# The softmax division of the second cross attention moves from GpSimd to VectorE, and the instruction orders from the experts on are new

## The chip, the cores and the metric

One Trainium2 chip, one core of it. The metric is the device time of the whole program in microseconds (us), median of the runs shown. The engines are TensorE (PE in the profile, PEld its weight loads), VectorE (DVE), ScalarE (ACT), GpSimd (POOL) and SyncE (SP).

## The reference

Sixteen sequences of 64 tokens with 128 features pass six blocks, each a layer norm, a function and a residual add. The context has 64 tokens of 96 features per sequence. The change touches the fifth block, whose function stands in full below.

```python
def reference(...):
    def _L1_xattn_ref(x, context, mask, W_q, W_k, W_v, W_o, b_o):   # HEADS = 8, DIM_HEAD = 64
        q = (x @ W_q).reshape(b, n, HEADS, DIM_HEAD)
        k = (context @ W_k).reshape(b, j, HEADS, DIM_HEAD)
        v = (context @ W_v).reshape(b, j, HEADS, DIM_HEAD)
        sim = jnp.einsum('bihd,bjhd->bhij', q, k) * scale
        sim = jnp.where(mask[:, None, None, :], sim, max_neg)
        attn = jax.nn.softmax(sim, axis=-1)
        out = jnp.einsum('bhij,bjhd->bihd', attn, v).reshape(b, n, INNER)
        return out @ W_o + b_o
    ...
    x = x + _L0_attn_ref(_layernorm(x, axis=-1), ...)    # causal attention, 16 heads
    x = x + _L0_xattn_ref(_layernorm(x, axis=-1), ...)   # cross attention, one head
    x = x + _L0_ffn_ref(_layernorm(x, axis=-1), ...)     # 8 experts (top 2) and a shared one
    x = x + _L1_attn_ref(_layernorm(x, axis=-1), ...)    # linear state recurrence, GELU, norm
    x = x + _L1_xattn_ref(_layernorm(x, axis=-1), ...)   # the function above
    x = x + _L1_ffn_ref(_layernorm(x, axis=-1), ...)     # 8 experts, each takes its best tokens
    return x
```

## The kernel before

The 1024 tokens are NT = 8 tiles of 128 rows, in two halves of HT = 4 tiles. `X` holds the residual stream, tile by tile, in SBUF, for the whole program; `XT` is the normalized input of a block, transposed. Every engine runs one list of steps, written out by hand at the end of its block (PE from L1100, ACT from L1569, DVE from L2132, POOL from L539), and each step waits on counting semaphores for what it needs. Nothing reorders these lists: a step that waits holds up every later step of its engine. Loads of weights are issued by SP long before they are used.

Every layer norm is spread over three engines: `ln_moments` (DVE, statistics of four tiles), `root` (POOL, the inverse root, L448), `ln_apply` (DVE, four tiles, L1828), `transpose_xn` (PE, L660) and `copy_xt` (ACT, L1380).

The second cross attention has, for each half, four `queries1` products (L970, copied by ACT at L1528 to `Q1T`), and for each tile t of the eight the following cycle:

1. `scores1` (PE): 4 products that write the mask bias (L988) and 32 small ones (L996) fill two PSUM banks; tile t waits until the maximum of tile t-2 is subtracted (`c_sub`).
2. `subtract_max1` (DVE): maximum of each row and head (L2030), then subtraction from PSUM into `Es` (L2033). `Es` has three buffers, so from t = 3 on the subtraction waits for the transposes of tile t-3 (`c_tr`).
3. `exponentials1` (ACT, L1532), in place in `Es`.
4. `probs1` (DVE): sums (L2041) and their reciprocal (L2042). It signals `c_sum`.
5. `weigh_probs` (POOL, L537): `Es` times the reciprocal, in place, 128 partitions by 512. It signals `c_prob`. Between tiles 2 and 3 POOL has `add_bias(0)` and `add_bias(1)` (L532), which add the output bias to the residual stream, once it is normalized (`xn_ready`).
6. `transpose_probs1` (PE, L1006, one bank), `copy_probs1` (ACT, L1538, into `PTs`), `weigh_values1` (PE, L1020), `copy_values1` (ACT, L1545, two copies into `V2`), `project_out` (PE, L1033, one bank) and `add1` (DVE, L2047), which waits for `bo_added` and releases the bank for the next tile.

After the eighth tile come the last layer norm and the second set of experts: `up1` (L1048), `gelu` (L1553), `down1` (L1060), `copy_ys` (L1561) and `add_expert` (DVE, L2119). Between them PE makes sixteen `count` products (L1087) for a search on DVE (`route`, from L2061) that finds which tokens an expert takes. `search_bits` (L2052) prepares shifted constants for it in half of `PTs`.

The program has `mask_row` (DVE, L1876) too, which turns the context mask into the row that L988 multiplies. It runs while the first experts compute.

Of the kernel before, what the change touches and what calls it, by code (L numbers as in the profile page):

```python
# [5 lines left out]
def decoder_kernel(nc: bass.Bass, w, out):  # L6
# [8 lines left out]
    ALU = mybir.AluOpType  # L15
# [41 lines left out]
    with ctx:  # L57
# [3 lines left out]
        def sem(name):  # L61
            return ctx.enter_context(nc.semaphore(name))

        def per_row(ap, n):

            return ap.unsqueeze(2).broadcast_to([ap.shape[0], ap.shape[1], n])
# [244 lines left out]
        c_sum = sem("c_sum")  # L311
# [132 lines left out]
        def _(pool):  # L444
# [89 lines left out]
            def weigh_probs(t):  # L534
                pool.wait_ge(c_sum, t + 1)
                e = Es[:, t % 3, :].rearrange("p (a s) -> p a s", s=S)
                nc.gpsimd.tensor_tensor(e, e, per_row(sm[:, t, 2, :], S), ALU.mult).then_inc(c_prob, 1)  # L537

# [82 lines left out]
            weigh_probs(0)  # L621
            weigh_probs(1)
            weigh_probs(2)
            add_bias(0)
            add_bias(1)
            weigh_probs(3)
            weigh_probs(4)
            weigh_probs(5)
            weigh_probs(6)
            weigh_probs(7)  # L630
# [6 lines left out]
        def _(pe):  # L637
# [252 lines left out]
            def up0_first(h, e):  # L890
                i = (E0 + 1) * h + e
                if i == 0:
                    pe.wait_ge(ld_f0, 128)
                    pe.wait_ge(kv_ready, 5)
                if e == 0:
                    pe.wait_ge(xt_ready[h], 3)
                if i >= 2:
                    pe.wait_ge(f_silu, i - 1)
                mm(bank[i % 2][:, :], W1a[:, e, :], XT[:, half(h)], start=True, stop=True).then_inc(f_h1, 1)  # L899

            def up0_third(h, e):
                i = (E0 + 1) * h + e
                if e == 0:
                    pe.wait_ge(xt_ready[h], 3)
                if i == 0:
                    pe.wait_ge(ld_f0, 128)
                    pe.wait_ge(a_sub, NU)
                if i == 1:
                    pe.wait_ge(kv_ready, 6)
                if i >= 2:  # L910
                    pe.wait_ge(f_h, i - 1)
                mm(bank[2 + i % 2][:, :], W3a[:, e, :], XT[:, half(h)], start=True, stop=True).then_inc(f_h3, 1)  # L912
# [42 lines left out]
            def read_out(h):  # L955
                pe.wait_ge(s_state[h], ROUNDS + 1)
                if h == 1:
                    pe.wait_ge(s_gelu[0], 1)
                mm(bank[6][:, :], ST[:, h, :, :].rearrange("p b s -> p (b s)"),
                   CT[:, :, :].rearrange("p q d -> p (q d)"), start=True, stop=True).then_inc(s_y[h], 1)  # L960
# [273 lines left out]
            up0_third(1, 6)  # L1234
            up0_first(1, 7)
            down0(1, 5)
            up0_third(1, 7)
            down0(1, 6)
            up0_first(1, 8)
            down0(1, 7)  # L1240
            up0_third(1, 8)
# [6 lines left out]
            read_out(0)  # L1248
            transpose_xn(3, 1, 6)
            keys_values1(9)  # L1250
# [3 lines left out]
            widen(1, 1)  # L1254
            widen(1, 2)
            keys_values1(11)
# [15 lines left out]
            transpose_probs1(0)  # L1272
            queries1(1, 1)
            queries1(1, 2)
            queries1(1, 3)
            scores1(3)
# [13 lines left out]
            project_out(3)  # L1290
            transpose_probs1(4)
            scores1(7)
            weigh_values1(4)
            transpose_probs1(5)
            project_out(4)
            transpose_probs1(6)
            weigh_values1(5)
            weigh_values1(6)
# [76 lines left out]
        def _(act):  # L1375
# [304 lines left out]
            weigh0(1, 3)  # L1680
            silu(1, 5)
            silu(1, 6)
            copy_xt(3, 0, 7)
            weigh0(1, 4)
            silu(1, 7)
            weigh0(1, 5)
            weigh0(1, 6)
            silu(1, 8)
# [3 lines left out]
            copy_xt(3, 1, 6)  # L1692
            state(1, 0)
            state(1, 1)
            keys_values1(8)
            keys_values1(9)
            state(1, 2)
# [6 lines left out]
            keys_values1(14)  # L1704
            copy_xt(4, 0, 0)
            queries1(0, 0)
            queries1(0, 1)
            keys_values1(15)
# [3 lines left out]
            copy_xt(4, 1, 6)  # L1712
            queries1(1, 0)
            copy_probs1(0)
            queries1(1, 1)
            exponentials1(1)
            queries1(1, 2)
            queries1(1, 3)
            exponentials1(2)
# [11 lines left out]
            copy_probs1(4)  # L1731
            copy_values1(4)
            copy_probs1(5)
            exponentials1(7)
            copy_probs1(6)
# [7 lines left out]
            copy_xt(5, 1, 6)  # L1743
            route_exp()
# [3 lines left out]
            copy_ys(0, 0)  # L1748
            copy_ys(0, 1)
# [3 lines left out]
            copy_ys(1, 0)  # L1753
            gelu(2, 0, 0)
            gelu(2, 1, 0)
            gelu(2, 0, 1)
# [36 lines left out]
        def _(dve):  # L1793
# [243 lines left out]
            def probs1(t):  # L2037

                dve.wait_ge(c_exp, t + 1)
                e = Es[:, t % 3, :].rearrange("p (a s) -> p a s", s=S)  # L2040
                then(V.tensor_reduce(sm[:, t, 1, :], e, AX.X, ALU.add))  # L2041
                V.reciprocal(sm[:, t, 2, :], sm[:, t, 1, :]).then_inc(c_sum, 1)  # L2042
# [132 lines left out]
            subtract_max(14)  # L2175
            subtract_max(15)
# [47 lines left out]
            mask_row()  # L2224
# [26 lines left out]
            probs1(0)  # L2251
            subtract_max1(1)
            subtract_max1(2)
            probs1(1)
# [13 lines left out]
            subtract_max1(7)  # L2268
            add1(4)
            ln_moments(5, 0)  # L2270
# [3 lines left out]
            add1(6)  # L2274
            add1(7)
            ln_moments(5, 1)
            ln_apply(5, 1)
            search_bits()
# [35 lines left out]
```

## Time and profile before

| | us |
|---|---|
| median of 3 runs | 254.05 |
| lowest and highest run | 252.47, 254.1 |
| the profiled execution, its own time | 255.0 |
| its span, first to last instruction | 253.3 |
| TensorE's mean granted clock over the span | 0.987 |

The span in forty slices of 6.3 us, as the page prints it (busy tenths of each engine; PEclk the granted clock in tenths of full speed):

```
PE   8997899889899999999988986999798999999995
DVE  5462899775949525454438999378755788778995
ACT  0756698943435859755862564575555635434360
POOL 4898900010200847439583122072411000000000
PEclk9999999999999999999999997699999999999999
```

A digit is the share of its slice in which the engine ran. The second cross attention lies at 155 to 188 us of the span, slices 25 to 30; the second experts follow to 247 us. Busy time of PE says that something was in its pipe, not that it ran at its peak. Of the idle times of the other engines only those count that a later step of PE had to wait for.

### The profile page before, as it was taken

Reading aid. Unit: us, or ns where it says so; the run is one execution under the profiler, and the core shown is the slowest. Engines: PE = TensorE matmul, PEld = TensorE weight load, DVE = VectorE, ACT = ScalarE, POOL = GpSimd, SP = SyncE. Lnnn points to the kernel's source line nnn. Section 1 sums busy time; section 2 is a strip of 40 time slices with the busy share of each in tenths; the row PEclk is TensorE's granted clock in tenths of the full one; section 3 lists DMA queues with packets and bytes.
Section 4 is the critical chain, followed back from the end, with each engine's and each line's share of the span. In section 5 each row is a group of like instructions: output and inputs, shape, how many; then the busy total and the mean of one; then the engine's idle time right before and its main releaser. Section 6 shows DMA issues by size and latency. Waiting matters only on the chain.

```text
span 253.3 us, 5539 instructions
## 1 busy us (share of the span) xinstructions
PE 233.2 (92%) x2018; PEld 158.3 (63%) x2018; DVE 172.1 (68%) x574; ACT 142.5 (56%) x297; POOL 79.0 (31%) x137
## 2 busy tenths in 40 slices
PE   8997899889899999999988986999798999999995
PEld 8555677654455666656664534497677575579765
DVE  5462899775949525454438999378755788778995
ACT  0756698943435859755862564575555635434360
POOL 4898900010200847439583122072411000000000
PEclk9999999999999999999999997699999999999999
DMA  5898950326700000000000000000000000000002
GB/s 135 174 199 243 308 153 27 107 83 169 211 0 0 5 0 0 1 0 3 0 1 3 1 0 3 0 3 5 1 3 1 3 0 0 0 4 0 3 0 83
DMA packets 22343, 12.23 MB, mean 48 GB/s; under 512 B 11320, under 2 KB 21309, under 8 KB 22317
## 3 DMA queue, kind: packets, MB, share of 16 engines
q1 hardware_dynamic: 21277, 11.53, 16.6%
q0 software_dynamic: 80, 0.20, 0.9%
q8 instruction: 16, 0.26, 0.4%
q10 hardware_dynamic: 960, 0.16, 0.3%
q14 instruction: 10, 0.08, 0.1%
HBM read 8.74 MB, written 3.15 MB: 47 GB/s over the span
## 4 chain that ended last, share of the span: by engine, by line
PE 37%; DVE 12%; POOL 2%; ACT 2%; issue 1%; DVEq 0%
PE bank L1048 11%; PE bank L1060 10%; PE bank L931 2%; PE bank L1033 2%; PE bank L970 2%; PE bank L912 2%; DVE stats L1806 2%; PE bank L899 1%; PE bank L1006 1%; PE bank L1020 1%; DVE sm L2030 1%; DVE XN L2006 1%; DVE XN L1828 1%; POOL Es L537 1%; POOL rs L448 1%
## 5 line engine op out<-in xcount | busy, mean ns | idle before, releaser
L448 POOL TENSOR_TENSOR rs<-rs,halves 128x4 f32<-128x4 f32 x14 | 14.3, 1023 | 78.2 <-DVE rs L1821 62.3
L524 POOL TENSOR_TENSOR X<-X,att 128x128 f32<-128x128 f32 x72 | 30.7, 464 | 13.0 <-ACT att L1513 13.0
L1048 PE MATMUL bank<-XT,Wb 128*128 128x512 f32 x64 | 29.6, 597 | 0.0
L1981 DVE SCALAR_TENSOR_TENSOR att<-bank,cols,att 128x512 f32<-128x512 f32 x18 | 13.5, 749 | 22.6 <-ACT att L1502 16.6
L1060 PE MATMUL bank<-Wb,att 128*128 128x128 f32 x224 | 27.4, 278 | 0.0
L1060 PEld LDWEIGHTS bank<-Wb,att 128*128 128x128 f32 x224 | 25.9, 192 | 1.5 <-issue 0.8
L1553 ACT ACTIVATE att<-bank 128x512 f32<-128x512 f32 x32 | 18.0, 600 | 8.3 <-PE bank L1048 8.0
L1513 ACT ACTIVATE att<-bank,comb 128x128 f32<-128x128 f32 x72 | 20.3, 381 | 4.0 <-PE bank L931 4.0
L931 PEld LDWEIGHTS bank<-W2a,att 128*128 128x128 f32 x144 | 18.2, 191 | 6.3 <-issue 4.3
L1502 ACT ACTIVATE att<-bank,cols 128x512 f32<-128x512 f32 x18 | 12.6, 699 | 12.8 <-DVE att L1981 7.4
L1561 ACT ACTIVATE big<-bank 128x512 f32<-128x512 f32 x14 | 8.4, 597 | 18.8 <-PE bank L1060 18.8
L931 PE MATMUL bank<-W2a,att 128*128 128x128 f32 x144 | 18.9, 278 | 0.0
L899 PE MATMUL bank<-XT,W1a 128*128 128x512 f32 x36 | 18.3, 603 | 0.0
L912 PE MATMUL bank<-XT,W3a 128*128 128x512 f32 x36 | 18.2, 595 | 0.0
L1828 DVE TENSOR_SCALAR XN<-X,mv,rs 128x128 f32<-128x128 f32 x48 | 14.1, 356 | 5.2 <-POOL rs L448 4.9
L1048 PEld LDWEIGHTS bank<-XT,Wb 128*128 128x128 f32 x64 | 11.3, 191 | 10.0 <-issue 8.4
L2119 DVE SCALAR_TENSOR_TENSOR X<-big,rt,X 128x128 f32<-128x128 f32 x56 | 15.4, 347 | 0.8 <-ACT big L1561 0.6
L537 POOL TENSOR_TENSOR Es<-Es,sm 128x512 f32<-128x512 f32 x8 | 8.3, 1044 | 17.6 <-DVE sm L2042 17.5
L1380 ACT ACTIVATE XT<-bank 128x512 f32<-128x512 f32 x12 | 7.2, 604 | 9.1 <-PE bank L660 9.1
L1916 DVE TENSOR_REDUCE mx<-bank 128x8 f32<-128x512 f32 x16 | 10.4, 684 | 2.0 <-PE bank L771 2.0
L1806 DVE BATCH_NORM_STATS2 stats<-X 128x6 f32<-128x128 f32 x48 | 10.4, 279 | 1.7 <-DMA X<-in_x 1.5
L660 PE MATMUL bank<-ident,XN 128*128 128x128 f32 x48 | 10.1, 308 | 1.3 <-ACT QKVT L1523 0.7
(229 smaller groups left out, 472.6 us busy)
## 6 DMA issues: line engine op xcount, KB each, us to landing
o_scratch<-big SPq DMA_DIRECT2D x2, 512.0 KB, 2.9
Wb<-in_L_ffn_W SPq DMA_DIRECT2D x1, 1024.0 KB, 5.4
Wb<-in_L_ffn_W SPq DMA_DIRECT2D x8, 128.0 KB, 5.2
X<-in_x SPq DMA_DIRECT2D x2, 256.0 KB, 3.0
k_scratch<-QKVT SPq DMA_DIRECT2D x1, 512.0 KB, 4.0
q_scratch<-QKVT SPq DMA_DIRECT2D x1, 512.0 KB, 5.2
Wb<-k_scratch SPq DMA_DIRECT2D x1, 512.0 KB, 4.4
v_scratch<-QKVT SPq DMA_DIRECT2D x1, 512.0 KB, 7.0
```

Source lines behind the costliest of these rows:

```text
L448: nc.gpsimd.tensor_tensor(rs[:, 0, cut], rs[:, 1, cut], halves[:, :], ALU.pow).then_inc(l_root[h], 1)
L524: nc.gpsimd.tensor_tensor(X[:, h * HT + t, :], X[:, h * HT + t, :], part0[:, i % 2, t, :], ALU.add).then_inc(f_acc, 1)
L899: mm(bank[i % 2][:, :], W1a[:, e, :], XT[:, half(h)], start=True, stop=True).then_inc(f_h1, 1)
L912: mm(bank[2 + i % 2][:, :], W3a[:, e, :], XT[:, half(h)], start=True, stop=True).then_inc(f_h3, 1)
L931: last = mm(bank[4 + i % 2][:, t * P:(t + 1) * P], hid0[:, i % 2, t * P:(t + 1) * P], W2a[:, e, :], start=not shared, stop=True, skip_grou ...
L1048: mm(bank[i % 4][:, :], W1b[:, e, f * P:(f + 1) * P], XT[:, half(h)], start=True, stop=True).then_inc(m_up, 1)
L1060: last = mm(bank[4 + h][:, t * P:(t + 1) * P], hid[:, e % 2, f, tile], W2b[:, e, f, :], start=(f == 0), stop=(f == F1 - 1))
L1513: AF(part0[:, i % 2, t, :], bank[4 + i % 2][:, t * P:(t + 1) * P], ACT.Copy, scale=comb[:, tt, e:e + 1]).then_inc(f_part, 1)
L1553: AF(hid[:, e % 2, f, half(h)], bank[i % 4][:, :], ACT.Gelu).then_inc(m_gelu, 1)
L1806: last = V.bn_stats(stats[:, t, :], src[:, t, :])
L1828: V.tensor_scalar(XN[:, t, :], X[:, t, :], mv[:, t, 0:1], rs[:, 0, t:t + 1], ALU.subtract, ALU.mult).then_inc(xn_ready[h], 1)
L2119: last = V.scalar_tensor_tensor(X[:, t, :], ys[:, e, t, :], rt[:, 9, t, e:e + 1], X[:, t, :], ALU.mult, ALU.add)
```

## The change

In the cycle of a tile, step 5 disappears from POOL, and `probs1` on DVE gets a third instruction: it waits for the reciprocal (`then`) and multiplies `Es` by it, and signals `c_prob`. The semaphore `c_sum` goes. POOL's list then has the two `add_bias` steps directly behind `root(5, 1)`. The lists of PE, ACT and DVE are changed in their order in several places, without a step added or removed: among the last steps of the first experts, among the context's keys and values (`keys_values1(9)`, `(11)`, `(15)`), in the cycle of the second cross attention, and in ACT's first copies of the second experts (`copy_ys(0, 0)` and `(0, 1)`). DVE makes `mask_row` in the first attention, between the last two `subtract_max`, and `search_bits` before `add1(7)`.

```diff
--- before.py
+++ after.py
@@ -308,7 +308,6 @@
         c_sub = sem("c_sub")
         c_exp = sem("c_exp")
         bo_added = sem("bo_added")
-        c_sum = sem("c_sum")
         c_prob = sem("c_prob")
         c_tr = sem("c_tr")
         c_trc = sem("c_trc")
@@ -530,11 +529,6 @@
                 pool.wait_ge(xn_ready[h], 5 * HT)
                 rows = X[:, h * HT:(h + 1) * HT, :]
                 nc.gpsimd.tensor_tensor(rows, rows, per_col(bo[:, :], HT), ALU.add).then_inc(bo_added, 1)
-
-            def weigh_probs(t):
-                pool.wait_ge(c_sum, t + 1)
-                e = Es[:, t % 3, :].rearrange("p (a s) -> p a s", s=S)
-                nc.gpsimd.tensor_tensor(e, e, per_row(sm[:, t, 2, :], S), ALU.mult).then_inc(c_prob, 1)
 
             root(1, 0)
             root(1, 1)
@@ -618,16 +612,8 @@
             root(5, 0)
             root(4, 1)
             root(5, 1)
-            weigh_probs(0)
-            weigh_probs(1)
-            weigh_probs(2)
             add_bias(0)
             add_bias(1)
-            weigh_probs(3)
-            weigh_probs(4)
-            weigh_probs(5)
-            weigh_probs(6)
-            weigh_probs(7)
             root(6, 0)
             root(6, 1)
         C_MISC = 7 + E0 + 2 + 1 + 2
@@ -1232,13 +1218,13 @@
             up0_first(1, 5)
             up0_first(1, 6)
             up0_third(1, 6)
+            up0_third(1, 7)
+            down0(1, 5)
             up0_first(1, 7)
-            down0(1, 5)
-            up0_third(1, 7)
+            up0_first(1, 8)
             down0(1, 6)
-            up0_first(1, 8)
+            up0_third(1, 8)
             down0(1, 7)
-            up0_third(1, 8)
             inject(0)
             down0(1, 8)
             widen(0, 0)
@@ -1246,14 +1232,14 @@
             widen(0, 2)
             keys_values1(8)
             read_out(0)
+            keys_values1(9)
             transpose_xn(3, 1, 6)
-            keys_values1(9)
             inject(1)
             widen(1, 0)
             keys_values1(10)
             widen(1, 1)
+            keys_values1(11)
             widen(1, 2)
-            keys_values1(11)
             read_out(1)
             keys_values1(12)
             keys_values1(13)
@@ -1269,10 +1255,10 @@
             scores1(2)
             transpose_xn(4, 1, 6)
             queries1(1, 0)
-            transpose_probs1(0)
             queries1(1, 1)
             queries1(1, 2)
             queries1(1, 3)
+            transpose_probs1(0)
             scores1(3)
             weigh_values1(0)
             scores1(4)
@@ -1288,13 +1274,13 @@
             weigh_values1(3)
             scores1(6)
             project_out(3)
+            scores1(7)
             transpose_probs1(4)
-            scores1(7)
+            transpose_probs1(5)
             weigh_values1(4)
-            transpose_probs1(5)
-            project_out(4)
             transpose_probs1(6)
             weigh_values1(5)
+            project_out(4)
             weigh_values1(6)
             project_out(5)
             transpose_probs1(7)
@@ -1678,23 +1664,23 @@
             silu(1, 4)
             weigh0(1, 2)
             weigh0(1, 3)
+            copy_xt(3, 0, 7)
             silu(1, 5)
             silu(1, 6)
-            copy_xt(3, 0, 7)
             weigh0(1, 4)
+            weigh0(1, 5)
             silu(1, 7)
-            weigh0(1, 5)
+            silu(1, 8)
             weigh0(1, 6)
-            silu(1, 8)
             weigh0(1, 7)
             weigh0(1, 8)
             gelu_states(0)
             copy_xt(3, 1, 6)
+            keys_values1(8)
             state(1, 0)
             state(1, 1)
-            keys_values1(8)
+            state(1, 2)
             keys_values1(9)
-            state(1, 2)
             state(1, 3)
             gelu_states(1)
             keys_values1(10)
@@ -1702,21 +1688,21 @@
             keys_values1(12)
             keys_values1(13)
             keys_values1(14)
+            keys_values1(15)
             copy_xt(4, 0, 0)
             queries1(0, 0)
             queries1(0, 1)
-            keys_values1(15)
             queries1(0, 2)
             queries1(0, 3)
             exponentials1(0)
             copy_xt(4, 1, 6)
+            exponentials1(1)
             queries1(1, 0)
-            copy_probs1(0)
             queries1(1, 1)
-            exponentials1(1)
+            exponentials1(2)
             queries1(1, 2)
             queries1(1, 3)
-            exponentials1(2)
+            copy_probs1(0)
             copy_values1(0)
             copy_probs1(1)
             exponentials1(3)
@@ -1729,10 +1715,10 @@
             exponentials1(5)
             exponentials1(6)
             copy_probs1(4)
+            copy_probs1(5)
             copy_values1(4)
-            copy_probs1(5)
+            copy_probs1(6)
             exponentials1(7)
-            copy_probs1(6)
             copy_values1(5)
             copy_values1(6)
             copy_probs1(7)
@@ -1741,18 +1727,18 @@
             gelu(0, 0, 0)
             gelu(0, 1, 0)
             copy_xt(5, 1, 6)
+            copy_ys(0, 0)
             route_exp()
             gelu(0, 0, 1)
             gelu(0, 1, 1)
             gelu(1, 0, 0)
-            copy_ys(0, 0)
-            copy_ys(0, 1)
             gelu(1, 1, 0)
             gelu(1, 0, 1)
             gelu(1, 1, 1)
-            copy_ys(1, 0)
             gelu(2, 0, 0)
             gelu(2, 1, 0)
+            copy_ys(0, 1)
+            copy_ys(1, 0)
             gelu(2, 0, 1)
             gelu(2, 1, 1)
             copy_ys(1, 1)
@@ -2039,7 +2025,8 @@
                 dve.wait_ge(c_exp, t + 1)
                 e = Es[:, t % 3, :].rearrange("p (a s) -> p a s", s=S)
                 then(V.tensor_reduce(sm[:, t, 1, :], e, AX.X, ALU.add))
-                V.reciprocal(sm[:, t, 2, :], sm[:, t, 1, :]).then_inc(c_sum, 1)
+                then(V.reciprocal(sm[:, t, 2, :], sm[:, t, 1, :]))
+                V.tensor_tensor(e, e, per_row(sm[:, t, 2, :], S), ALU.mult).then_inc(c_prob, 1)
 
             def add1(t):
                 dve.wait_ge(bo_added, t // HT + 1)
@@ -2173,6 +2160,7 @@
             row_max(14)
             row_max(15)
             subtract_max(14)
+            mask_row()
             subtract_max(15)
             sums_inverse(0)
             add_attention(0)
@@ -2221,7 +2209,6 @@
             gate0(1, 5)
             gate0(1, 6)
             gate0(1, 7)
-            mask_row()
             gate0(1, 8)
             state(0, 0)
             state(0, 1)
@@ -2248,9 +2235,9 @@
             ln_moments(4, 1)
             subtract_max1(0)
             ln_apply(4, 1)
-            probs1(0)
             subtract_max1(1)
             subtract_max1(2)
+            probs1(0)
             probs1(1)
             probs1(2)
             subtract_max1(3)
@@ -2266,16 +2253,16 @@
             probs1(5)
             probs1(6)
             subtract_max1(7)
+            ln_moments(5, 0)
             add1(4)
-            ln_moments(5, 0)
             probs1(7)
             add1(5)
             ln_apply(5, 0)
             add1(6)
+            search_bits()
             add1(7)
             ln_moments(5, 1)
             ln_apply(5, 1)
-            search_bits()
             route()
             add_expert(0)
             add_expert(1)
```

## Rows read from the trace of the kernel before

**Rows 1.** page, part 1: busy microseconds, share of the span, instructions

```profile
PE 233.2 (92%) x2018; PEld 158.3 (63%) x2018; DVE 172.1 (68%) x574; ACT 142.5 (56%) x297; POOL 79.0 (31%) x137
```

**Rows 2.** windows: start:end, length, busy and (count) per engine, clock, DMA

```profile
153.00:156.00 3.00, 1.58 (x80) 1.44 (x84) 2.90 (x13) 1.35 (x2) 1.01 (x1) 0.90 0.02 5
159.00:162.00 3.00, 3.00 (x7) 1.65 (x8) 1.09 (x2) 0.90 (x2) 0.00 (x0) 0.50 0.00 0
180.00:182.00 2.00, 1.23 (x37) 0.92 (x36) 1.74 (x11) 1.60 (x4) 0.00 (x0) 1.00 0.00 0
200.00:225.00 25.00, 25.00 (x139) 16.74 (x139) 19.91 (x85) 10.86 (x20) 0.00 (x0) 1.00 0.00 1
```

**Rows 3.** chain that ended last, in order of time: start, us, what

```profile
170.49 1.05 POOL Es L537
```

**Rows 4.** timeline of PE, second cross attention: start, us, engine line operation, count

```profile
158.73 2.07 PE L970 MATMUL bank<-XT,Wq 128*128 128x512 f32 x2 [0.69 <-ACT XT L1380]
...
164.61 0.30 PE L988 MATMUL bank<-maskrow,onesb 64*64 64x256 bf16 x4
...
168.13 0.69 PE L1020 MATMUL bank<-PTs,big 64*64 64x64 f32 x32
168.65 0.29 PE L988 MATMUL bank<-maskrow,onesb 64*64 64x256 bf16 x4
...
169.33 0.66 PE L1006 MATMUL bank<-ident,Es 128*128 128x128 f32 x4
169.83 1.06 PE L1033 MATMUL bank<-Wo,V 128*128 128x128 f32 x8
170.81 0.69 PE L1020 MATMUL bank<-PTs,big 64*64 64x64 f32 x32
...
178.54 0.66 PE L1006 MATMUL bank<-ident,Es 128*128 128x128 f32 x4 [0.52 <-POOL Es L537]
...
182.09 0.69 PE L1020 MATMUL bank<-PTs,big 64*64 64x64 f32 x32 [0.87 <-ACT V L1545]
...
187.95 1.88 PE L1048 MATMUL bank<-XT,Wb 128*128 128x512 f32 x4
```

**Rows 5.** timeline of DVE, second cross attention

```profile
164.05 0.69 DVE L2041 TENSOR_REDUCE sm<-Es 128x8 f32<-128x512 f32 x1 [3.93 <-ACT Es L1532]
...
174.71 0.69 DVE L2030 TENSOR_REDUCE sm<-bank 128x8 f32<-128x512 f32 x1 [0.87 <-PE bank L996]
175.43 0.69 DVE L2033 TENSOR_TENSOR Es<-bank,sm 128x512 f32<-128x512 f32 x1
...
176.44 0.69 DVE L2041 TENSOR_REDUCE sm<-Es 128x8 f32<-128x512 f32 x1
177.16 0.20 DVE L2042 RECIPROCAL sm<-sm 128x8 f32<-128x8 f32 x1
...
180.40 0.86 DVE L1806 BATCH_NORM_STATS2 stats<-X 128x6 f32<-128x128 f32 x4
...
181.79 0.68 DVE L2041 TENSOR_REDUCE sm<-Es 128x8 f32<-128x512 f32 x1
```

**Rows 6.** groups of ACT lines in 155:188: count, busy, mean ns, idle before

```profile
L1545 ACT ACTIVATE V<-bank 128x256 f32<-128x256 f32 x16 | 5.3, 381 | 5.1 <-PE bank L1020 5.0
L1532 ACT ACTIVATE Es<-Es 128x512 f32<-128x512 f32 x8 | 5.0, 626 | 2.6 <-DVE Es L2033 2.5
```

**Rows 7.** timeline of DVE in the first cross attention

```profile
64.44 0.69 DVE L1933 TENSOR_TENSOR X<-XN,X 128x512 f32<-128x512 f32 x1
```

**Rows 8.** timeline of DVE: four-tile normalizations beside and without GpSimd adds

```profile
113.42 1.71 DVE L1828 TENSOR_SCALAR XN<-X,mv,rs 128x128 f32<-128x128 f32 x4 [1.14 <-POOL rs L448]
...
155.58 1.10 DVE L1828 TENSOR_SCALAR XN<-X,mv,rs 128x128 f32<-128x128 f32 x4
```

**Rows 9.** timeline of DVE around the mask row, its new and old place

```profile
51.04 0.56 DVE L1911 RECIPROCAL rO<-bank 128x64 f32<-128x64 f32 x1 [1.10 <-PE bank L819]
...
124.97 0.68 DVE L1876 TENSOR_SCALAR maskrow<-masku 128x1024 bf16<-128x1024 uint8 x1
```

## The prediction, made before the changed kernel ran

> **What bounds the kernel now.** I read the page's busy times first: TensorE has work in its pipe for 92% of the span, DVE for 68%, POOL for 31% [rows 1]. By itself that says only that the end is set by what TensorE waits for or has to do. The windows say where which of the two holds [rows 2]. From 200 to 225 TensorE is busy for all of its 25.00 us at full clock: the second experts are a block of TensorE work that starts when the cross attention lets it, and that I take as rigid. In the second cross attention it is different: TensorE ran 1.23 of the 2 us from 180 to 182, and 1.58 of 3 from 153 to 156, and in 159:162 it ran at half of its clock, 1.2 instead of 2.4 GHz, after the thin stretch before. So the metric moves by what the change does to the moment at which the first up product of the second experts starts, 187.95 [rows 4]. The chain of waits then tells what reaches that moment: it goes through the eight-tile cycle, twice over the GpSimd multiply, once as the 1.05 us shown [rows 3], and otherwise over TensorE, DVE and ACT's copies. The timelines of TensorE and DVE give the steps: how far apart two starts lie when nothing waits. All my arithmetic below goes by such distances.
>
> **The price of each step.** TensorE [rows 4]: value products 168.13 to 168.65, 0.52; scores 168.65 to 169.33, 0.68; probability transposes 169.33 to 169.83, 0.50; output projection 169.83 to 170.81, 0.98. Behind its last issue each has a drain of some 0.16 (transposes: 0.66 long, 0.50 apart) before ACT can read. DVE [rows 5]: a maximum 0.72 to its subtraction (174.71 to 175.43); subtraction and one residual add together 1.01 (175.43 to 176.44), which I split as 0.68 and 0.33; a sum 0.72 to its reciprocal; the four statistics and what follows them 1.39 (180.40 to 181.79). ACT [rows 6]: exponential 0.63, the two value copies 5.3 over eight tiles, 0.66.
>
> **The multiply itself.** POOL loses eight of 1.05 us. DVE gets eight with 128x512 f32, both inputs in SBUF. The same shape with both inputs in SBUF, the residual add of the first cross attention, took 0.69 [rows 7]; here one input is broadcast over 64 columns, as in the subtraction of rows 5, which also took 0.69. I take 0.69, and 0.22 from the reciprocal's start to the multiply's (the reciprocal is 0.20 long). From the reciprocal to the transposes it was about 0.20 + 0.07 + 1.05 + 0.05 = 1.37, and will be 0.22 + 0.69 + 0.04 = 0.95: each tile is ready 0.42 earlier, if DVE comes to it as early as before. But DVE is held about 0.22 + 0.65 - 0.12 = 0.75 longer for each tile, 6.0 for eight. That is covered where DVE was idle, as in the 3.93 and the 0.87 of rows 5, and uncovered where it runs through, as over tiles 5 to 7.
>
> **The cycle, walked through in the new order.** Up to the third score tile TensorE's list of this stage is the old one, and so is DVE's, which reaches it at 154; the half clock stays. The query products and the first transposes swap places, the same work up to the fourth scores, which start at 164.5 (164.61 before). DVE meanwhile has its first three subtractions done at 159.3, multiplies tile 0 by 161.0 and tile 1 by 162.4, and waits for the third exponential, now behind one query copy fewer: tile 2 is ready at 165.25. Where 3.93 us of idle stood, two multiplies now go: no cost.
>
> From there TensorE: scores 3 at 164.5, values 0 at 165.35, scores 4 165.9, transposes 1 166.55, projection 0 167.05, values 1 168.0, scores 5 168.55, transposes 2 169.2, projection 1 169.7, values 2 170.7, transposes 3 171.2, then it waits for ACT's value copy (behind the exponential of tile 4): projection 2 172.1, values 3 173.1, scores 6 173.6, projection 3 174.5, scores 7 175.5, transposes 4 176.15. The transposes of tiles 1 to 3 meet ready tiles (162.4, 165.25, 170.05), so the 0.42 is not spent, and this half is as dense in TensorE as before. DVE: maximum 6 cannot start before 174.5 (174.71 before), since scores 6 end there.
>
> Then DVE sets the pace: add 3 until 176.1, tile 5 with its multiply ready at 177.75, tile 6 at 179.3, subtraction 7 until 180.65, the statistics of the first half 180.55 to 181.95, add 4, tile 7 from 182.2 and ready at 183.8. TensorE: transposes 5 at 177.8, values 4 178.3, transposes 6 179.35, values 5 179.85, projection 4 180.4; values 6 waits for a value copy that stands behind exponential 7 on ACT (180.65 + 0.63 + 0.66): 181.95; projection 5 182.45, transposes 7 183.85, projection 6 184.4, values 7 185.4, four layer-norm transposes 185.95, projection 7, after the value copy, 186.9, first up product **187.85**. Before: 187.95. Two multiplies (tiles 5 and 6) delay subtraction 7 by about 1.5, and the two earlier score tiles, the latency and the new order give it back: a sum of **-0.1 us**. Its error I put at 0.7 either way, a step or two of 0.5 to 0.98.
>
> **What is moved elsewhere.** `mask_row`, 0.68 [rows 9], goes before the last subtraction of the first attention: that ends near 50.6 instead of 49.95, and DVE's next instruction waited 1.10 us until 51.04 [rows 9], so it is covered, as is the exponential behind it; without this cover it would cost 0.68. At 125 it leaves a gap, no gain. `search_bits` goes into DVE's wait for projection 7, of 2 us; the projection ends at 188, so its 1.3 us are covered. The end of the first experts is TensorE without idle in other order: the gates it needs come 0.05 us or more before their products in my walk, 0. `keys_values1(9)` and `(11)` change places with idle stretches of 0.7 and 0.4 whose far side waits for the same ACT copies, 0; the DVE chain of norm and state sets the end of that stage. `copy_ys(0, 0)` goes where ACT waits; `(0, 1)` is needed only by a down product some 2 us later: 0. No DMA is moved or added, and no queue of SP or POOL is passed by one.
>
> **The two bias adds** now start when `root(5, 1)` ends, at 155.5, beside DVE's `ln_apply(4, 1)` at 155.58. Four such instructions took 1.71 beside GpSimd adds and 1.10 without [rows 8]: price 0.6, between 0 and the 1.3 of a whole bias add. Taken at 0.6 it delays the second maximum to 157.2, and its exponential is not due on ACT before 158.7: 0 in the sum. The Trainium skill, SBUF — State Buffer, section "SBUF: two separate sides", has it harder: such a pair of instructions excludes each other, and the one that starts first blocks the other for its whole length. By that rule all four wait until 156.8, the layer-norm transposes behind them end 0.15 later, and the sum would be +0.05 instead of -0.1. The row with 1.71 speaks rather for taking turns, since POOL had work through all of it.
>
> **Rivals.** (a) The latency is what counts: every tile's 0.42 is on the chain, as it would be if the chain went from multiply to transpose in each tile. TensorE waited for POOL for 0.52 at 178.54 [rows 4]; against it, the chain goes over POOL only twice. Eight tiles give -3.4: 250.7. Related to it, and counted with it: the half clock of 159:162 sits after a thin stretch, and a run in which it does not fall saves half of the 3.5 us of TensorE work at that clock and of the 2 before: -2.5. Together 18%. (b) Slower: the wait of TensorE at 176.65 to 177.8 in my walk, behind transposes 4, then 0.5, 0.55 and 0.4 at 178.8, 181.4 and 183.45. The clock fell once, after 153:156 with half of the time idle [rows 2]; if the new, thinner stretch 176.6 to 183.8 makes it fall, some 6 us run at half of it, of which three quarters or so were work: +2.8, 256.9. [...] Against it: 180:182 with 0.77 of 2 us idle kept 1.00 [rows 2], 182.09 came after 0.87 of waiting [rows 4]. 15%, with an uncovered DVE (tiles 4 to 7 each 0.75 late, +3.0 less what the latency gives) in it. (c) It does nothing beyond a few tenths, my forecast, 67%.
>
> **How the numbers follow.** The profiled execution had a span of 253.3 and a time of 255.0, 0.95 above the median of 254.05 and above all three runs. -0.1 gives 254.9 for such an execution and **253.9** for the median. The three runs themselves lie 1.6 apart, so 1%, 2.5 us, is what I count as a difference. The forecast's own range is 253.0 to 255.0 by the walk's error; stretched towards (a) and (b), where a part of either is as likely as all of it, 251.2 to 256.5. Outside remain about 2 in 10. Faster 18%, within 1% 67%, slower 15%.
>
> **What would show it.** Right: L537 gone, a third instruction of `probs1` at 0.69 (eight, DVE at 177.6 busy, POOL at 70.7), the first up product within 0.7 of 187.85, transposes 5 and 7 waiting for DVE, the half clock at 155 to 162 as before. Wrong: a multiply of 0.9 or more; the fourth scores away from 164.5; a granted clock below 1 after 165; any idle in TensorE within the second experts, which I hold rigid; the last subtraction of the first attention ending after 51.0.

## The result, and the profile after

The changed kernel took 255.54 us (median of 15 runs, 253.49 to 256.45), the old one beside it 252.59 (15 runs, 252.46 to 255.5). The ratio of the means is 1.0086 with a 95% interval of 1.0055 to 1.0117: slower by 0.9%, clear of noise, though under 2%. (The ratios below are of means too.) I had forecast no change, 253.9.

Both kernels fall into groups of runs, told apart by the mean clock that TensorE was granted over the run. In the profiled executions it is 1.000 (to within 0.001) where the clock stayed at 2.4 GHz through the second cross attention, and about 0.993 or 0.987 where it was at 1.2 for a while. I group the other runs by the same numbers. All numbers below keep these groups apart (medians; the old kernel's from the 103 runs beside the experiments):

| mean clock | old kernel | changed kernel | difference |
|---|---|---|---|
| 1.000 | 252.57 (50 runs) | 253.56 (2 runs) | 1.0 |
| 0.993 | 254.19 (30) | 255.24 (3) | 1.05 |
| 0.987 | 255.25 (23) | 256.17 (10) | 0.9 |

So there are two losses: about 1.0 us in every group, and a move between groups: half of the old kernel's runs keep the clock, two of the changed kernel's fifteen do. Weighted by these counts the groups give means 2.0 us apart, so each loss is about half of the whole. The old kernel's group sizes vary too: its median was 252.65 in one set of 34 runs and 254.05 in one of 35. Both profiled executions, old and new, are of the group at 0.987.

The changed kernel's profiled execution took 256.45, its span 254.7. Page, part 1, answering to [rows 1]; the multiplies have left POOL (79.0 to 70.3) and are on DVE (172.1 to 179.4):

```profile
PE 233.8 (92%) x2017; PEld 157.9 (62%) x2018; DVE 179.4 (70%) x582; ACT 143.2 (56%) x297; POOL 70.3 (28%) x129
```

TensorE's timeline, answering to [rows 4]: `scores1(2)`, the layer-norm transposes, the four query products, the scores of tile 3, the transposes of tiles 5 and 6 with their waits for DVE, those of tile 7, and the first up product.

```profile
155.86 0.30 PE L974 MATMUL bank<-maskrow,onesb 64*64 64x256 bf16 x4 [1.41 <-DVE Es L2019]
...
156.95 1.16 PE L646 MATMUL bank<-ident,XN 128*128 128x128 f32 x4 [0.32 <-DVE XN L1814]
158.79 6.61 PE L956 MATMUL bank<-XT,Wq 128*128 128x512 f32 x8 [0.69 <-ACT XT L1366]
...
165.77 0.30 PE L974 MATMUL bank<-maskrow,onesb 64*64 64x256 bf16 x4
...
179.26 0.66 PE L992 MATMUL bank<-ident,Es 128*128 128x128 f32 x4 [0.86 <-DVE Es L2029]
...
180.83 0.66 PE L992 MATMUL bank<-ident,Es 128*128 128x128 f32 x4 [0.28 <-DVE Es L2029]
...
185.31 0.66 PE L992 MATMUL bank<-ident,Es 128*128 128x128 f32 x4
...
189.31 1.88 PE L1034 MATMUL bank<-XT,Wb 128*128 128x512 f32 x4
```

The scores of tile 3 start at 165.77 instead of 164.61 and the first up product at 189.31 instead of 187.95. Of the 1.36 us, 1.16 are there before the cycle begins to run, 0.2 come in its tail. Behind the up product nothing changed: 65.4 us to the end of the span in both (254.7 - 189.31, 253.3 - 187.95). 0.14 of the 1.16 are older than the stage: `scores1(2)` starts at 155.86 instead of 155.72.

DVE's timeline, answering to [rows 5] and [rows 8], and under it POOL's over the same stretch:

```profile
155.72 1.94 DVE L1814 TENSOR_SCALAR XN<-X,mv,rs 128x128 f32<-128x128 f32 x4
157.58 0.68 DVE L2016 TENSOR_REDUCE sm<-bank 128x8 f32<-128x512 f32 x1
...
161.17 0.69 DVE L2029 TENSOR_TENSOR Es<-Es,sm 128x512 f32<-128x512 f32 x1
...
163.76 0.69 DVE L2027 TENSOR_REDUCE sm<-Es 128x8 f32<-128x512 f32 x1 [0.34 <-ACT Es L1518]
...
166.61 0.69 DVE L2016 TENSOR_REDUCE sm<-bank 128x8 f32<-128x512 f32 x1 [1.20 <-PE bank L982]
...
184.56 0.69 DVE L2029 TENSOR_TENSOR Es<-Es,sm 128x512 f32<-128x512 f32 x1
```

```profile
155.54 1.27 POOL L531 TENSOR_TENSOR X<-X,bo 128x512 f32<-128x512 f32 x1
157.74 1.26 POOL L531 TENSOR_TENSOR X<-X,bo 128x512 f32<-128x512 f32 x1 [0.93 <-DVE XN L1814]
```

The four instructions of `ln_apply(4, 1)` take 1.94 instead of the 1.10 of [rows 8]. The group of that line alone shows how (minimum, median, maximum of the four, in ns):

```profile
L1814 DVE TENSOR_SCALAR XN<-X,mv,rs x4: 332/334/1171, 155.7 to 157.3; 128x128 f32<-128x128 f32 x4
```

Three of them take 0.33; one takes 1.17. It is the first, which alone fills DVE from 155.95 to 156.5: bias add 0 began on POOL 0.18 us ahead of it, at 155.54, and ended at 156.81, and the DVE instruction ended just behind it, at 156.9. The second add, from 157.74, ran beside DVE instructions that read PSUM (L2016 at 157.58); they took their usual 0.68 and 0.69. The multiply is 0.69, as forecast.

The windows, answering to [rows 2]; first the new execution, then one row of the old. The low clock lasts from 157.8 to 164.7 in the new, from 155.4 to 162.2 in the old:

```profile
155.00:157.00 2.00, 0.82 (x37) 0.69 (x37) 1.97 (x4) 0.63 (x1) 1.81 (x2) 1.00 0.00 0
157.00:158.00 1.00, 1.00 (x4) 0.50 (x4) 1.00 (x4) 0.00 (x0) 0.26 (x1) 0.92 0.00 0
...
159.00:162.00 3.00, 3.00 (x4) 1.26 (x5) 2.90 (x6) 1.23 (x2) 0.00 (x0) 0.50 0.00 0
162.00:164.50 2.50, 2.50 (x4) 0.97 (x3) 2.06 (x5) 1.30 (x3) 0.00 (x0) 0.50 0.00 0
165.00:168.00 3.00, 2.96 (x111) 2.35 (x110) 1.76 (x4) 1.74 (x4) 0.00 (x0) 1.00 0.00 0
```

```profile
162.00:162.50 0.50, 0.50 (x2) 0.19 (x1) 0.00 (x0) 0.29 (x1) 0.00 (x0) 0.78 0.00 0
```

So this pair doesn't show the blocked instruction directly. The first query product starts only 0.06 later (158.79, before 158.73): the old transposes ran at the low clock, the new ones at full clock. From there to tile 3's scores it takes 6.98 instead of 5.88, because the low stretch, 6.8 to 6.9 us in both, now lies on all of the query products. What the blocked instruction costs has to be read at full clock.

### The profile page after: what moved, and what is told of

Read it like the earlier page. It is cut to its first block, busy times and chain, and to the rows that moved or that the text cites. A ratio compares the mean times of both kernels' runs of the same rounds, so it can differ in the third digit from the quotient of the medians.

```text
span 254.7 us, 5537 instructions
## 1 busy us (share of the span) xinstructions
PE 233.8 (92%) x2017; PEld 157.9 (62%) x2018; DVE 179.4 (70%) x582; ACT 143.2 (56%) x297; POOL 70.3 (28%) x129
## 4 chain that ended last, share of the span: by engine, by line
PE 38%; DVE 13%; issue 1%; ACT 1%; POOL 1%; DVEq 0%
PE bank L1034 11%; PE bank L1046 10%; PE bank L956 3%; PE bank L917 2%; PE bank L1019 2%; DVE stats L1792 2%; PE bank L898 2%; PE bank L885 1%; DVE XN L1814 1%; PE bank L1006 1%; DVE mv L1795 1%; DVE XN L1992 1%; PE bank L992 1%; PE bank L1073 1%; POOL rs L447 1%
## 5 line engine op out<-in xcount | busy, mean ns | idle before, releaser
L1814 DVE TENSOR_SCALAR XN<-X,mv,rs 128x128 f32<-128x128 f32 x48 | 14.9, 373 | 4.6 <-POOL rs L447 4.4
L956 PE MATMUL bank<-XT,Wq 128*128 128x512 f32 x16 | 10.4, 810 | 1.4 <-ACT XT L1366 1.4
```

The costliest lines, as they stand in the source:

```text
L956: mm(bank[4 + 2 * h + i % 2][:, :], Wq1[:, i * P:(i + 1) * P], XT[:, half(h)], start=True, stop=True).then_inc(c_q[h], 1)
L1814: V.tensor_scalar(XN[:, t, :], X[:, t, :], mv[:, t, 0:1], rs[:, 0, t:t + 1], ALU.subtract, ALU.mult).then_inc(xn_ready[h], 1)
```

## The experiments

Theories: **D**, DVE's extra instructions are the loss; **C**, it is only TensorE's clock; **O**, the new orders cost it, and **P**, of these the new tail of the cycle; **K**, the two bias adds, which now run beside `ln_apply(4, 1)`; **S**, my walk holds at the half clock of the profile, but at full clock DVE's extra steps lie bare.

**1 and 2. The two halves of the change alone.** Run 1: new orders, POOL multiplies (the semaphore and `weigh_probs` itself return too).

```diff
                 then(V.tensor_reduce(sm[:, t, 1, :], e, AX.X, ALU.add))
-                then(V.reciprocal(sm[:, t, 2, :], sm[:, t, 1, :]))
-                V.tensor_tensor(e, e, per_row(sm[:, t, 2, :], S), ALU.mult).then_inc(c_prob, 1)
+                V.reciprocal(sm[:, t, 2, :], sm[:, t, 1, :]).then_inc(c_sum, 1)
...
+            weigh_probs(0)
+            weigh_probs(1)
+            weigh_probs(2)
             add_bias(0)
             add_bias(1)
+            weigh_probs(3)
...
+            weigh_probs(7)
```

> The changed kernel with its new orders, but GpSimd multiplies again as before (POOL: tiles 0 to 2, the two bias adds, tiles 3 to 7). Theory D, DVE's longer occupation costs the time: the median comes back to the old kernel's 252.6 or goes below it, 251.5 to 252.9. Theory C, only the clock (a fall of TensorE's clock at 155 to 165 has become more frequent and its low stretch lies later, because the bias adds now collide with ln_apply(4, 1)): the collision is gone here too, so 252.6 as well, but then the clean runs without a fall gain nothing against the changed kernel's 253.5. Theory O, the new orders cost the time: it stays at 253.5 or more.

Run 2 is the opposite: the old kernel with this edit the other way round.

> The old kernel with its old orders, but DVE multiplies. Theory D: slower than the old one by 1 us or more, 253.6 to 255, since the first multiply stands before the second maximum. Theory C: the same collision of bias add and ln_apply as in the changed kernel, so as many low-clock runs, 255.2 to 256.4. Theory O: 252.6, no loss.

Measured: run 1 253.5, ratio to the old kernel 1.0018 (0.9979 to 1.0057); at full clock 253.42 (7 of 12 runs). Run 2 256.87 over all 12; four of these, near 258.9 at a mean clock of 0.979, are left out of its ratio, 1.0095 (1.005 to 1.0141; the other eight have 256.6); at full clock 254.77 (2 of 12). That is above every value I had expected for it. At full clock the four kernels are: old orders on POOL 252.57, on DVE 254.77; new orders on POOL 253.42, on DVE 253.56. So neither D nor O alone: the new orders cost 0.85 with the multiply on POOL, and take 1.2 off with it on DVE (two runs at full clock on each side of that last comparison; runs 10 and 5 below repeat it). And few runs keep the clock where DVE multiplies, which is also where the bias adds come early; these two had to be separated.

**3 and 4. The clock held.** Six products into a free PSUM bank where TensorE waits 1.4 us for the first subtraction, in the old and in the changed kernel:

```diff
             scores1(1)
+            for _ in range(6):
+                mm(bank[7][:, :], perm[:, :], causal[:, :, :].rearrange("p a k -> p (a k)"), start=True, stop=True)
             scores1(2)
```

> The old kernel with six extra products of 512 columns into a free PSUM bank between scores1(1) and scores1(2), where TensorE idles 1.4 us at 154.3: no granted clock below 1.00 there. All theories: the best case of the old kernel, 252.5, with no runs at 254 to 255.5.

> The changed kernel with the same six extra products. Theory C: with the clock held, it equals the old filled one, 252.5 (within 0.3). Theory D: it stays 1 us slower at the same clock, 253.5, and all else it lost (253.5 to 255.5) was the clock.

Measured: run 3 252.55, all 12 runs between 252.42 and 252.93 at full clock, ratio to the old kernel 0.996 (0.9932 to 0.9988). It beats both kernels on average, and equals the old one's runs at full clock. Run 4 253.77; eight of 12 at full clock with 253.69, the others at 255.24. Theory C falls as the whole cause: at the same clock the changed kernel is 1.1 slower. In run 4's profiled execution the clock fell all the same, at 159, so filling the gap at 154.3 is not enough there.

**5 and 6. Where the 1.1 us are.** Run 5 adds three more such products behind `transpose_xn(4, 1)`. Run 6 has them too, and keeps the bias adds off `ln_apply(4, 1)`:

```diff
                 pool.wait_ge(xn_ready[h], 5 * HT)
+                pool.wait_ge(c_prob, 2)
                 rows = X[:, h * HT:(h + 1) * HT, :]
```

> The changed kernel with nine extra products: the six of before and three more behind transpose_xn(4, 1), where TensorE waits for the transposed half. Theory S (the walk was right at the half clock of the profile, but at full clock DVE's extra 0.75 per tile lies bare: TensorE reaches scores1(3) some 2 us earlier, DVE doesn't): all runs at clock 1.00, 253.6, 1.0 to 1.2 above the old kernel's clean 252.5, and subtract_max1(3) starts on DVE 2 us or more after scores1(3) ends on TensorE (in the old kernel filled, at once). Theory C (only the clock): 252.5.

> The same, and the bias adds wait until tile 1 is multiplied, so that they no longer run beside ln_apply(4, 1). If that collision (1.94 instead of 1.10 us for the four) is part of the bare DVE time, 0.8 less than the run before, 252.8; if DVE has slack there, 253.6 as before it.

Measured: run 5 253.71 (11 of 12 at full clock, with 253.70), run 6 253.24 (11 of 12, with 253.23). The collision thus costs at least 0.47 at full clock. TensorE's timelines at full clock, of run 3 (old), run 5 (changed) and run 6 (bias adds late); the first query product, the scores of tile 3, the first up product:

```profile
157.79 1.13 PE L970 MATMUL bank<-XT,Wq 128*128 128x512 f32 x2 [0.69 <-ACT XT L1382]
...
161.99 0.30 PE L988 MATMUL bank<-maskrow,onesb 64*64 64x256 bf16 x4
...
185.34 1.88 PE L1048 MATMUL bank<-XT,Wb 128*128 128x512 f32 x4
```

```profile
157.11 1.09 PE L646 MATMUL bank<-ident,XN 128*128 128x128 f32 x4 [0.33 <-DVE XN L1818]
...
158.89 3.80 PE L956 MATMUL bank<-XT,Wq 128*128 128x512 f32 x8
...
163.06 0.30 PE L974 MATMUL bank<-maskrow,onesb 64*64 64x256 bf16 x4
...
186.59 0.59 PE L1034 MATMUL bank<-XT,Wb 128*128 128x512 f32 x1
```

```profile
158.08 3.80 PE L957 MATMUL bank<-XT,Wq 128*128 128x512 f32 x8
...
162.24 0.30 PE L975 MATMUL bank<-maskrow,onesb 64*64 64x256 bf16 x4
...
186.19 1.02 PE L1035 MATMUL bank<-XT,Wb 128*128 128x512 f32 x2
```

Executions differ in when they reach this stage: `scores1(2)` starts at 155.75, 156.02 and 156.04. From there to the first query product it takes 2.04 in the old kernel, 2.87 in the changed one, 2.04 with the late bias adds. That is 0.83: the one blocked DVE instruction, 1.17 instead of 0.33. TensorE waits 0.33 for it ahead of the transposes and again inside them, and the transposes, the copy of `XT` and the first query product follow in line. From tile 3's scores to the first up product it is 23.35, 23.53 and 23.95. So the cycle itself costs 0.2 in the changed kernel, and in run 6 another 0.4: the run gains 0.47, not 0.8. DVE's timeline of run 6 shows what:

```profile
155.90 1.11 DVE L1819 TENSOR_SCALAR XN<-X,mv,rs 128x128 f32<-128x128 f32 x4
...
162.07 0.69 DVE L2034 TENSOR_TENSOR Es<-Es,sm 128x512 f32<-128x512 f32 x1
...
163.64 1.12 DVE L2034 TENSOR_TENSOR Es<-Es,sm 128x512 f32<-128x512 f32 x1
164.68 0.68 DVE L2021 TENSOR_REDUCE sm<-bank 128x8 f32<-128x512 f32 x1
```

```profile
L532 POOL TENSOR_TENSOR X<-X,bo x2: 1273/1496/1718, 162.9 to 164.2; 128x512 f32<-128x512 f32 x2
```

`ln_apply` is back at 1.11, but the third multiply, two inputs in SBUF, now lies beside the first bias add (from 162.94 on POOL, 1.27 long) and takes 1.12. Blocking goes both ways: the second add, at 164.2, took 1.72 beside that multiply. The maximum behind the multiply starts at 164.68, 1.7 after the scores of tile 3 ended (163.0).

Theory S as I put it doesn't come out. Its sign was that this maximum starts 2 us or more after the scores' end in run 5 and at once in the old kernel. Maximum 3 of run 3 and of run 5:

```profile
164.08 0.64 DVE L2032 TENSOR_REDUCE sm<-bank 128x8 f32<-128x512 f32 x1
```

```profile
165.06 0.68 DVE L2020 TENSOR_REDUCE sm<-bank 128x8 f32<-128x512 f32 x1
```

The scores end at 162.75 and 163.82: 1.3 in the old kernel, 1.2 in the changed one. The three moved multiplies up to here cost nothing even at full clock. DVE is merely late for these scores in both, so that a further 0.4 on the multiply isn't covered.

**7. The late bias adds, clock free.** The edit of run 6 without the extra products.

> The changed kernel unfilled with the late bias adds. Theory K (the collision makes TensorE's thin stretch thinner, so the clock falls in more runs): as many runs at clock 1.00 as the old kernel has, four to seven in ten, instead of two in fifteen, and a median of 253 to 254.5. If the collision has nothing to do with the clock: one or two runs in ten at 1.00, and 255.4.

Measured: 253.74, ratio 1.0025 (0.9989 to 1.0061); six of 12 at full clock, with 253.21 (changed kernel 253.56). So K for the clock, as far as six against two of 15 shows it, and for the first part of the loss at full clock; there 0.64 over the old kernel stays.

**8. What the new orders cost POOL.** Run 1, filled twice, with the old tail:

```diff
             project_out(3)
-            scores1(7)
             transpose_probs1(4)
-            transpose_probs1(5)
+            scores1(7)
             weigh_values1(4)
+            transpose_probs1(5)
+            project_out(4)
             transpose_probs1(6)
             weigh_values1(5)
-            project_out(4)
             weigh_values1(6)
```

(ScalarE's copies and exponential 7 accordingly.)

> The new orders with the multiply on GpSimd (the first run of this study), both gaps filled, and the tail of the cycle as in the old kernel: transposes 4 before scores 7, values 4 before transposes 5, projection 4 before transposes 6. Theory P (the new orders lose 0.9 of a clean run because DVE's add1(4) stands before probs1(7) and waits for a projection 4 that is now later): 252.5. If the loss is elsewhere in the orders: 253.4.

Measured: 252.6, at full clock 252.59 (11 of 12), ratio 0.999 (0.9967 to 1.0013). The 0.85 of run 1 is its tail, on TensorE and ScalarE; which wait in it makes the loss I haven't separated. All other moves (`mask_row`, keys and values, the first experts, the first half of the cycle, the copies of the second experts) cost and bring nothing together while POOL multiplies. With DVE multiplying they are worth 0.7: run 10 against run 11 below.

**9. The collision put into the old kernel.** Nothing but the order on POOL:

```diff
+            add_bias(0)
+            add_bias(1)
             weigh_probs(0)
             weigh_probs(1)
             weigh_probs(2)
-            add_bias(0)
-            add_bias(1)
```

> The old kernel, unfilled, with nothing changed but the two bias adds ahead of the first GpSimd multiply, so that they run beside ln_apply(4, 1) as in the changed kernel. Theory K (the collision is what the change lost): runs at clock 1.00 take 253.3 (0.8 more than 252.5), they become rare (one to three in ten instead of five), and the median is 255. If the collision costs a clean run nothing: 252.5 in clean runs. If it doesn't touch the clock: half of the runs at 1.00.

Measured: 255.05, ratio 1.0068 (1.0032 to 1.0103); two of 12 runs at full clock, with 253.77 and 254.47. The clock went as theory K had it, and the loss at full clock is more than its 0.8 (I had expected 253.3 for such runs): in the profiled execution the first transposes also wait 0.20 for POOL, whose first multiply stands behind both bias adds.

```profile
158.71 1.13 PE L970 MATMUL bank<-XT,Wq 128*128 128x512 f32 x2 [0.69 <-ACT XT L1380]
160.04 0.66 PE L1006 MATMUL bank<-ident,Es 128*128 128x128 f32 x4 [0.20 <-POOL Es L537]
```

**10 and 11. DVE multiplies with the old tail.** Run 10 is run 2, filled twice; run 11 the changed kernel, filled twice, with the edit of run 8.

> The second run of this study (old orders, DVE multiplies) with both gaps filled: 254.7, all at clock 1.00. Of the 2.2 over the old kernel 0.8 are the collision; in the trace the rest stands in the tail: values 6 wait for a value copy behind exponential 7, which waits for subtraction 7 behind two multiplies.

> The changed kernel, filled twice, with the old tail on TensorE and ScalarE (transposes 4, scores 7, values 4, transposes 5, projection 4; exponential 7 ahead of copy 6). If the new tail was what makes the DVE multiply bearable: 254.2 to 254.7, about 1 more than 253.7. If the old tail is better with either engine: below 253.4.

Measured: run 10 254.89 (at full clock 254.87, 8 of 12; I had expected all 12), run 11 254.24 (at full clock 254.13, 7 of 12; run 5 253.70). The old tail is 0.4 worse for DVE; I had expected about 1. What it costs is the wait named in the expectation, values 6 for a value copy behind exponential 7 (0.87 before, [rows 4]). In run 10, and with another result in run 11:

```profile
181.89 0.69 PE L1006 MATMUL bank<-PTs,big 64*64 64x64 f32 x32 [1.80 <-ACT V L1535]
```

```profile
181.16 0.89 PE L1006 MATMUL bank<-PTs,big 64*64 64x64 f32 x32 [1.79 <-ACT V L1535]
```

```profile
181.50:182.00 0.50, 0.50 (x26) 0.38 (x16) 0.43 (x3) 0.00 (x0) 0.31 (x1) 0.50 0.00 0
182.00:184.00 2.00, 2.00 (x12) 2.00 (x10) 0.47 (x1) 0.66 (x2) 0.00 (x0) 0.50 0.04 8
```

In run 11's profiled execution (mean clock 0.992) the clock stayed at 1.00 through 155 to 181.5 and fell in the tail, right behind that wait, to 0.50 from 181.5 to about 184.9. Five of its 12 runs are of that group, at 255.4. Run 10's profiled execution had the same wait and kept its clock.

**12. The bias adds behind the third multiply** (`c_prob, 3` in the edit of run 6).

> The changed kernel, filled twice, with the bias adds behind the third multiply. With them behind the second one (253.23) the third multiply took 1.12 instead of 0.69, two SBUF inputs beside a GpSimd add. If that is a bare 0.4: 252.8, and the rest over 252.5 is the tail's 0.2 to 0.3. If DVE has slack there: 253.2.

Measured: 252.79, all 12 between 252.64 and 252.93, ratio to the unfilled old kernel 0.9974 (0.9943 to 1.0006). `ln_apply` takes 1.10 and the third multiply 0.69:

```profile
155.78 1.10 DVE L1819 TENSOR_SCALAR XN<-X,mv,rs 128x128 f32<-128x128 f32 x4
...
163.52 0.69 DVE L2034 TENSOR_TENSOR Es<-Es,sm 128x512 f32<-128x512 f32 x1
164.13 0.68 DVE L2021 TENSOR_REDUCE sm<-bank 128x8 f32<-128x512 f32 x1
```

The clean sum at full clock closes: changed kernel 253.70; the collision with `ln_apply` and with the third multiply away, 252.79, so it cost 0.9; the 0.2 that remain to the filled old kernel's 252.55 are the 0.2 by which the cycle was longer in run 5, and is here too (first up product at 185.66, scores of tile 3 at 162.12: 23.54). Even without its collision the change brings nothing. With the new tail alone the DVE multiply is the better one (252.79 against 253.42 in run 1), but the best kernels here, 252.55 and 252.59, multiply on POOL with the old tail.

**The clock, counted over all filled kernels.** Where the bias adds stay off `ln_apply` (runs 3, 6, 8, 12), 46 of 48 runs kept it; where they collide (runs 4, 5, 10, 11), 34 of 48. Not all of these falls need to come from the collision: the one of run 11 that was profiled lay in the tail.

## Why the prediction was wrong

**The multiply** (right): 0.69 for each of eight, POOL 70.3 against a forecast of 70.7. DVE's busy time rose by 7.3 instead of 5.5; 0.8 of the rest is the blocked instruction, the remaining 1.0 is spread over many groups of instructions, none with more than 0.3.

**The cycle** (right within its error): from tile 3's scores to the first up product I had 187.85 - 164.5 = 23.35, against 23.54 measured in the profile. TensorE waited for DVE at the transposes of tiles 5 and 6, as walked; those of tile 7 got their input at 185.25, and started at 185.31. The new orders are what makes this so: at full clock it was 0.4 more with the old tail (run 11), and 1.2 more with all old orders (run 10, beside run 5).

**The two bias adds** (wrong, the step that failed): "Taken at 0.6 it delays the second maximum to 157.2, and its exponential is not due on ACT before 158.7: 0 in the sum." I followed DVE's next steps, and looked at the transposes only for the blocking rule, where I let a half-clocked TensorE hide it: before, the transposes took until 158.0 in any case. At full clock they end by 157.1 (run 3), and behind them `copy_xt` and the queries are the chain. The price there, put at 0, is 0.83 in the trace (runs 5 and 6) and 0.9 in the times (runs 5 and 12), and 0.4 falls on the third multiply if the adds are merely pushed behind the second. The clock also falls in more runs: with the early bias adds and no extra products 6 of 39 runs kept it (changed kernel, runs 2 and 9), without 63 of 127 (old kernel, runs 1 and 7). That the blocked instruction does this by stretching the thin part of TensorE's work fits, but no run shows it by itself.

**"The half clock stays"** (wrong as a premise): the profiled execution of before is of the slowest of three groups, and I took its half clock as fixed in being there and in its place, though it cost that execution 2.6 us at tile 3's scores (164.61, 161.99 in run 3) and the three runs shown were 1.6 apart. In the changed kernel's profiled execution it came 2.4 us later, and the fourth scores, walked to 164.5, started at 165.77; I had named that as a sign of being wrong. The cover that I counted, DVE's 3.93 us of idle, is the shadow of that half clock. In run 3 the same wait is 1.27. It was still enough for the first three multiplies.

```profile
161.43 0.69 DVE L2043 TENSOR_REDUCE sm<-Es 128x8 f32<-128x512 f32 x1 [1.27 <-ACT Es L1534]
```

**The blocking rule.** The Trainium skill (SBUF — State Buffer, "SBUF: two separate sides") has the instruction that starts first exclude the other for its whole length. The trace agrees: the first of four took 1.17 and ended with the bias add. I preferred the row with 1.71 for four, taking it for turn-taking [rows 8]; with adds of 0.42, and no single one of the old kernel's 48 such instructions above 0.49, blocking by the first to start and turns can't be told apart there. My sum by the rule, though, was +0.05, since it stood on the same half clock, and in the profiled pair the first query product did start only 0.06 later. So the rule alone would not have saved the forecast: the collision was priced at the wrong clock.

**What is moved elsewhere** (right): `mask_row` ran at 49.30 for 0.68 and the last subtraction ended at 50.58, and run 8 shows the sum of all other moves as 0 while POOL multiplies. The second experts were rigid, as held.

**Rivals:** (a) fell: run 12 against run 3 has the kernel with the shorter latency 0.24 slower, not 3.4 faster. (b) named a clock fall in the tail. The changed kernel's tail kept 1.00 in its profile, where the clock fell earlier, in a stretch that I had called constant; with the old tail run 11 shows just such a fall. Two prices don't follow from their own terms: half of 3.5 and 2 us is 2.75, not 2.5, and a half-clock stretch of 6 us, three quarters of it work, costs 2.25, not 2.8. Neither changes the forecast.

## What to carry to other kernels

When an engine's queue gets shorter, ask what now starts earlier on it and, where it is GpSimd, beside which VectorE instruction: here the moved multiply was nearly free with the new orders, and two adds that nobody touched cost 0.9 us at full clock. Before using an idle stretch as cover, check the granted clock in it; at full clock it may be a third as long. And where runs of one kernel lie in groups, compare group with group, then count how many fall in each.

## What I had not expected of the hardware

A GpSimd add of 128x512 (1.27 us) that began 0.18 us ahead of it held a VectorE `tensor_scalar` of 128x128, SBUF to SBUF, for 1.17 us instead of 0.33, and a VectorE multiply with both inputs in SBUF took 1.12 instead of 0.69 beside a like add. The blocking went the other way too: the add behind it took 1.72 beside that multiply. DVE instructions that read PSUM kept their 0.68 and 0.69 beside an add. Six products of 512 columns (0.21 us each) that compute nothing, in the one gap of the old kernel, kept the clock up in all 12 runs and made it 0.4% faster on average. In the changed kernel eight of 12 runs kept it with six such products and 11 with nine, too few runs to tell the two apart. A wait of 1.79 us in the cycle's tail was followed by 3.4 us at 1.2 GHz in run 11; a like wait in run 10 was not.
